# TensorE's turn re-ordered, and the routing counts moved to another PSUM bank

## The chip, the cores and the metric

The kernel runs on one core of a Trainium2 chip. The metric is the device time of one execution in microseconds (us), the median of three runs. The engines are named as the profile names them: PE (TensorE, matmuls), PEld (its weight loads), DVE (VectorE), ACT (ScalarE), POOL (GpSimd) and SP (the sync engine, which here issues DMAs).

## What is computed

The input holds 8 images of 16 x 16 tokens with 256 channels. Each image goes through a layer norm over channels, attention along rows and along columns (both of 16 tokens, the scores minus a squared distance) and an output projection, added to the image. Then 2048 tokens go through a mixture of 8 experts with one expert for each token: logits, argmax, a place in the expert's list of at most 256 tokens (the running count of earlier tokens that chose it), and an expert of 256 to 1024 to 256 with a ReLU, scaled by the gate and added.

```python
q, k, v = xn @ Wq.T + bq, xn @ Wk.T + bk, xn @ Wv.T + bv      # xn = layer norm of x
r = softmax(q.k along the row    - gw * dist) @ v
c = softmax(q.k along the column - gw * dist) @ v
x = x + (r + c) @ Wo.T + bo
t = layer norm of x; idx = argmax(t @ wg); mask = one_hot(idx)
loc = cumsum(mask, axis=0) - 1; mask = mask * (loc < C)       # C = 256
out = x + gate * (relu(t_e @ w1[e]) @ w2[e])                  # per expert e
```

## The kernel before

The program has three parts. A set-up (up to about 24 us) folds the weights. An attention part (about 24 to 76 us) takes the images one at a time, each as two tiles of 128 tokens. An expert part (from about 84 us) takes the experts one at a time. Products are made exact by splitting each operand into a high and a low part and running three passes (`three_passes`, lines 592 to 611), so each product needs a "high" copy from ACT and a "low" remainder from DVE.

Every engine has a queue written out by hand, in order, with semaphore waits between the engines. In the attention part one turn i (1 to 6) of the loop at L759 issues on PE:

- `transpose_x(i + 1)` (L622): the normalised image i+1 is transposed into `bank_xT`;
- `scores(i)`: needs the query of image i, high from ACT and low from DVE, and that DVE has read the previous scores;
- `transpose_prob(i - 1)` (L662): transposes the combined attention weights of image i-1 into `bank_pT`, after `weights_both(i - 1)` on DVE;
- `query(i + 1)`: needs the transposed image i+1, high from ACT, low from DVE (`x_low`);
- `counts(i - 2)` (L684 to L691): tiny matmuls that count earlier tokens by expert, into the tail of the bank `banks_v` half 0, after `choose(i - 2)` on DVE;
- `attention_out(i - 1, 0 and 1)` (L675): weights times values into `banks_o`;
- `values(i)`: values times output projection into `banks_v`, which needs ACT's copy of the values before and, as the counts lie in the same bank, that DVE has read the counts.

DVE's turn i (`turn`, L1235) is: `x_low(i + 1)` (L1118), `maxima(i)` for both tiles (L1170, L1173: masks the scores and takes their maxima), `place(i - 2)` (L1230 to L1233: reads the counts, gives `slot`), `first_norm(i + 4)` in turns 1 to 3 (L1105 to L1111: statistics of a later image), `weights_both(i)` (L1192 to L1196: reads the sums of ACT's exponentials, combines `e_col` and `e_row`), `query_low(i + 1)` (L1123), `residual(i - 1)` for both tiles (L1210: the new row of the output), and `choose(i - 1)` (L1218 to L1225: argmax of the logits, by way of `ranked` and `chosen`).

ACT's turn i (L977 to L987) is: `transposed_x(i + 1)`, `normalised_x(i + 2)`, `transposed_prob(i - 1)` (L916), `exponentials(i)` for both tiles (L929, L930), `query(i + 1)` (L910: the high part of the query), a piece of an expert's weights in some turns, `values(i)` (L936).

POOL's loop (L516) issues for image i: `pre_residual(i - 1)` (L466 to L470, four small operations), `x_and_bias(i)` (L476: image plus bias, which waits until `residual(i - 2)` has freed its buffer), in four turns a piece of `w1_low` (L492), `scatter_rows(i - 2)` (L483: two indirect DMAs that wait for `slot`), `sum_marks(i - 2)` (L502 to L505) and, while images are left, `first_rstd(i + 4)` (L428 to L431, which waits for `first_norm`). Ahead of the loop stand `x_and_bias(0)`, `pre_residual(0)`, `first_w1_low(2)`, `x_and_bias(1)`, `first_w1_low(3)` and `first_rstd(5)`; the first of these waits for `bias_rows` on DVE (L1164, L1165).

Of the kernel before, what the change touches and what calls it, by code (L numbers as in the profile page):

```python
# [39 lines left out]
E, F = 8, 1024  # L40
# [49 lines left out]
def wait(eng, sem, value):  # L90

    if isinstance(value, int) and value <= 0:
        return
    eng.wait_ge(sem, value)
# [18 lines left out]
def build(nc, x, Wq, bq, Wk, bk, Wv, bv, Wo, bo, sigma, wg, w1, w2, tables_in, eye, tokens, slots, out):  # L113
# [4 lines left out]
    with ctx:  # L118
# [93 lines left out]
        def halves(a):  # L212
            return a.rearrange("p (a b) -> p a b", a=2)
# [4 lines left out]
        ps_v, ps_o = two_banks("banks_v"), two_banks("banks_o")  # L218

        ps_count = halves(ps_v[:, 0, MW:MW + 2 * E])  # L220
        ps_x0 = [ps_q[:, 0, :], ps_s[:, 0, :]]
        ps_s_last = [ps_s[:, 0, :], ps_xT[:, 1, :]]
        ps_pT_last = [ps_pT, ps_q]
# [88 lines left out]

        def slot_of(i):
            return slot_last if i == B - 1 else slot[i % 2]


        def w1_high_count(e):
# [267 lines left out]
        def _(pe):  # L585
# [30 lines left out]
            def transpose_x(i):  # L616

                pe.wait_ge(xn_ready, i + 1)
                wait(pe, xT_ready, i)
                for t in range(2):  # L620
                    for c in range(DC):
                        step = nc.tensor.transpose(ps_xT[:, c, t * P:(t + 1) * P], xn[:, t, c * P:(c + 1) * P], ident)  # L622
                step.then_inc(xT_made, 1)
# [21 lines left out]
            def values(i, which=range(2)):  # L645

                j = i % 2
                wait(pe, v_ready, i)
                wait(pe, count_read, i - 1)
                for t in which:  # L650
                    step = three_passes(ps_v[:, t, 0:MW], [(xT_high[j][:, c, chunk[t]], xT_low[j][:, c, chunk[t]]) for c in range(DC)],
                                        [(m_high[:, c, :], m_low[:, c, :]) for c in range(DC)])
                    if t == 1 or i == B - 1:
                        step.then_inc(v_made, 1)

            def transpose_prob(i, which=range(2)):

                wait(pe, pT_ready, 2 * i)
                for t in which:
                    pe.wait_ge(u_ready, 2 * i + t + 1)  # L660
                    for c in range(2):
                        step = nc.tensor.transpose(pT_of(i, t)[:, c, t * P:(t + 1) * P], e_col[:, t, c * P:(c + 1) * P], ident)  # L662
                    step.then_inc(pT_made, 1)

            def attention_out(i, t, between=None):

                pe.wait_ge(pT_ready, 2 * i + (t + 1 if i == B - 1 else 2))
                pe.wait_ge(v_ready, i + 1 + (i == B - 1))
                wait(pe, x2_ready, 2 * (i - 1) + t + 1)
                if i == 0:  # L670
                    pe.wait_ge(b_ready, 1)
                for c in range(2):
                    if between and c:
                        between()
                    step = nc.tensor.matmul(ps_o[:, t, 0:VW], pT[:, c, t * P:(t + 1) * P], v_sb[i % 2][:, c, 0:VW], start=c == 0, stop=c == 1)  # L675
                step.then_inc(o_made, 1)

            def counts(i):

                pe.wait_ge(chosen_ready, i + 1)  # L680
                wait(pe, count_read, i)
                pe.wait_ge(v_ready, min(i + 2, B + 1))
                new, old = chosen_wide[i % 2], chosen_wide[1 - i % 2]
                nc.tensor.matmul(ps_count, ones[:, :], new[:, 0:2, :], start=True, stop=False)  # L684
                if i:
                    for t in range(2):
                        nc.tensor.matmul(ps_count, ones[:, :], old[:, 1 + t:2 + t, :].to_broadcast([P, 2, E]), start=False, stop=False)
                if i > 1:
                    pe.wait_ge(before_ready, i - 1)
                    nc.tensor.matmul(ps_count, ones[:, :], before[1 - i % 2][:, :].unsqueeze(1).to_broadcast([P, 2, E]), start=False, stop=False)  # L690
                nc.tensor.matmul(ps_count, upper, new[:, 1:3, :], start=False, stop=True).then_inc(count_made, 1)  # L691
# [16 lines left out]
            def fold_biases():  # L708

                pe.wait_ge(wide_ready, 1)  # L710
                for c in range(DC):
                    nc.tensor.matmul(ps_o[:, 1, 0:VW], bv_wide[:, c, :], woT[:, c, :], start=c == 0, stop=False)
                for c in range(DC):
                    step = nc.tensor.matmul(ps_ow, bo_wide[:, c, :], wgc[:, c, :], start=False, stop=c == DC - 1)
                step.then_inc(obias_made, 1)
# [40 lines left out]
            pe.wait_ge(m_ready, 1)  # L756
            values(0)
            fold_biases()
            for i in range(1, B - 1):  # L759
                transpose_x(i + 1)  # L760
                scores(i)
                transpose_prob(i - 1)
                query(i + 1)
                if i > 1:
                    counts(i - 2)
                attention_out(i - 1, 0)
                attention_out(i - 1, 1)
                values(i)


            transpose_prob(B - 2)
            scores(B - 1)
            counts(B - 3)
            attention_out(B - 2, 0)
# [100 lines left out]
        def _(act):  # L875
# [10 lines left out]
            def normalised_x(i):  # L886

                act.wait_ge(nmr_ready, x_group(i) + 1)
                wait(act, xT_made, i)
                for t in range(2):  # L890
                    r = 2 * i + t
                    step = nc.scalar.activation(xn[:, t, :], x_sb[:, r, :], ACT.Identity, scale=rstd[:, r:r + 1], bias=nmr[:, r:r + 1])
                step.then_inc(xn_ready, 1)
# [8 lines left out]
            def transposed_x(i):  # L902

                act.wait_ge(xT_made, i + 1)
                nc.scalar.activation(xT_high[i % 2][:, :, :], ps_xT, ACT.Copy).then_inc(xT_high_ready, 1)
# [27 lines left out]
            def values(i):  # L933
                act.wait_ge(v_made, i + 1)
                wait(act, pre_ready, i - 1)
                nc.scalar.activation(v_sb[i % 2][:, :, :], ps_v[:, :, 0:MW], ACT.Copy).then_inc(v_ready, 1)  # L936

            def second_w1_high(n):

                c, part = w1_piece(n)  # L940
                act.wait_ge(w1_in, 32)
                nc.scalar.activation(w1_high[1][:, c, part], w1_in_sb[:, c, part], ACT.Copy).then_inc(w1_high_ready, 1)
# [30 lines left out]
            normalised_x(2)  # L973
            query(1)
            values(0)
            for i in range(1, B - 1):
                transposed_x(i + 1)  # L977
                if i + 2 < B:
                    normalised_x(i + 2)
                transposed_prob(i - 1)  # L980
                exponentials(i)
                query(i + 1)
                if i + 1 in W1_TURNS:
                    second_w1_high(i + 1 - W1_TURNS[0])
                if i == B - 2:
                    split_w2(0, which=[0])
                values(i)  # L987


            def last_values(t):  # L990
# [98 lines left out]
        def _(dve):  # L1089
# [26 lines left out]
            def x_low(i):  # L1116
                dve.wait_ge(xT_high_ready, i + 1)
                low_part(xT_low[i % 2][:, :, :], ps_xT, xT_high[i % 2][:, :, :]).then_inc(xT_ready, 1)  # L1118
# [43 lines left out]
            def bias_rows():  # L1162
                dve.wait_ge(obias_made, 1)
                setup.mark(nc.vector.tensor_copy(ow[:, :], ps_ow))  # L1164
                nc.vector.tensor_tensor(obias[:, :], ps_obias, bo_sb[:, :], ALU.add).then_inc(b_ready, 1)  # L1165
# [61 lines left out]
            def place(i, target):  # L1227

                dve.wait_ge(count_made, i + 1)
                nc.vector.tensor_tensor(counted[:, :, :], ps_count, chosen[i % 2], ALU.mult).then_inc(count_read, 1)  # L1230
                dve.wait_ge(count_read, i + 1)
                route.done(nc.vector.tensor_reduce(loc[:, :], counted[:, :, :], axis=AX.X, op=ALU.add))
                return nc.vector.scalar_tensor_tensor(target[:, :], loc[:, :], float(E), rmax[:, :], ALU.mult, ALU.subtract)  # L1233

            def turn(i):  # L1235
                x_low(i + 1)
                maxima(i, 0)
                maxima(i, 1)
                if i > 1:
                    place(i - 2, slot_of(i - 2)).then_inc(slot_ready, 1)  # L1240
                if i < 4:
                    first_norm(i + 4)
                weights_both(i)
                query_low(i + 1)
                residual(i - 1, 0)
                residual(i - 1, 1)
                choose(i - 1)
# [9 lines left out]
            first_norm(4)  # L1257
            weights_both(0)
            query_low(1)
            bias_rows()  # L1260
            for i in range(1, B - 1):
                turn(i)
# [145 lines left out]
```

## Time and profile before

| what | us |
|---|---|
| median of 3 runs | 190.01 (190.01 to 190.08) |
| the profiled execution, its own time | 189.76 |
| its span, first to last instruction | 187.9 |
| PE busy | 175.9 (94%) |
| DVE busy | 147.6 (79%) |
| POOL busy | 119.6 (64%) |
| ACT busy | 112.8 (60%) |

The profiled execution lies 0.25 us under the median, and 1.86 us of it lie outside the span. In a timeline row the columns are: start (us from the span's start), length (us), engine, line, operation, output and inputs with their tile names, sizes, and the number of merged instructions; in square brackets the idle time before it and what ended it. The length of one row may reach a little into the next, since instructions overlap; the distance between starts is what a step takes of its engine's queue.

### The profile page before, as it was taken

The numbers are of one execution on the slowest core, as the hardware profiler recorded it, in microseconds if no ns is written. First come the engines' busy times: TensorE is split into PE (matmuls) and PEld (weight loads), VectorE is DVE, ScalarE is ACT, GpSimd is POOL, SyncE is SP. The second block draws the span as 40 slices with busy tenths as digits, with TensorE's granted clock in tenths as the row PEclk, the third lists the DMA queues.
The fourth block names the chain that finished last, engine by engine and source line by source line (L and its number), as shares of the span: only waits on it lengthen the run. The fifth ranks groups of instructions, "written<-read, shape, count | busy, mean of one in ns | idle before, by whom it ended". The sixth has DMA issues, their size and how long they took to land.

```text
span 187.9 us, 3937 instructions
## 1 busy us (share of the span) xinstructions
PE 175.9 (94%) x1370; PEld 168.8 (90%) x1370; DVE 147.6 (79%) x400; ACT 112.8 (60%) x273; POOL 119.6 (64%) x159
## 2 busy tenths in 40 slices
PE   7899999799999999989899899999999999999980
PEld 7788898699899999769899899999999999999970
DVE  1397979998987978755867889999699996997820
ACT  0647966578679488523659795791875926845000
POOL 4226778278877967828349688748468494369562
PEclk9999999999999999999999999999999999999996
DMA  5896997611312124769299629139184193601010
GB/s 169 244 368 226 301 258 205 234 61 58 112 36 85 58 86 124 244 179 304 53 330 356 236 79 390 36 127 345 62 284 162 63 348 145 205 22 45 5 68 30
DMA packets 23862, 31.67 MB, mean 169 GB/s; under 512 B 2729, under 2 KB 20650, under 8 KB 23841
## 3 DMA queue, kind: packets, MB, share of 16 engines
q1 hardware_dynamic: 20032, 26.01, 42.5%
q0 software_dynamic: 1616, 4.24, 6.4%
q10 hardware_dynamic: 2192, 1.16, 2.1%
q8 instruction: 11, 0.18, 0.4%
q14 instruction: 11, 0.08, 0.1%
HBM read 23.02 MB, written 8.55 MB: 168 GB/s over the span
## 4 chain that ended last, share of the span: by engine, by line
PE 65%; DVE 12%; DMA 10%; issue 5%; ACT 4%; SPq 2%; POOLq 1%; POOL 0%; DVEq 0%
PE banks_v L603 8%; PE banks_v L604 7%; PE banks_v L610 7%; DMA w_in_sb<-in_L_ffn_w 6%; PE banks_o L675 4%; PE bank_q L610 3%; PE bank_pT L610 3%; PE bank_pT L603 3%; PE bank_pT L604 3%; PE bank_s L610 3%; PE bank_s L603 3%; PE bank_s L604 3%; PE bank_q L603 3%; PE bank_q L604 3%; DMA slots<-row,slot 2%
## 5 line engine op out<-in xcount | busy, mean ns | idle before, releaser
L950 ACT ACTIVATE w_high<-w_in_sb 128x1024 fp32r<-128x1024 f32 x22 | 22.9, 1057 | 4.2 <-DMA w_in_sb<-in_L_ffn_w 4.0
L560 POOL DMA_INDIRECT out<-y,goal x16 | 16.7, 1041 | 11.6 <-issue 5.8
L483 POOL DMA_INDIRECT slots<-row,slot x14 | 14.3, 1023 | 14.7 <-DVE slot L1233 8.8
L542 POOL TENSOR_TENSOR w_low<-vx,w_high 128x1024 fp32r<-128x1024 f32 x8 | 20.1, 2532 | 5.2 <-ACT w_high L950 5.2
L542 POOL TENSOR_TENSOR w_low<-w_in_sb,w_high 128x1024 fp32r<-128x1024 f32 x7 | 16.7, 2409 | 9.7 <-ACT w_high L950 9.6
L1322 DVE TENSOR_TENSOR w_low<-w_in_sb,w_high 128x1024 fp32r<-128x1024 f32 x12 | 15.8, 1317 | 5.1 <-ACT w_high L950 4.7
L603 PE MATMUL banks_v<-w_high,h_high 128*128 128x256 f32 x64 | 16.3, 291 | 0.5 <-issue 0.5
L675 PE MATMUL banks_o<-vx,pT 128*128 128x266 f32 x64 | 16.4, 397 | 0.3 <-issue 0.3
L1048 ACT ACTIVATE h_high<-bank_xT 128x512 fp32r<-128x512 f32 x8 | 4.8, 594 | 18.6 <-PE bank_xT L610 18.6
L604 PE MATMUL banks_v<-w_high,h_low 128*128 128x256 f32 x64 | 15.8, 283 | 0.0
L603 PE MATMUL bank_pT<-w_high,h_high 128*128 128x256 f32 x56 | 14.0, 287 | 0.0
L604 PE MATMUL bank_pT<-w_high,h_low 128*128 128x256 f32 x56 | 13.7, 283 | 0.0
L675 PEld LDWEIGHTS banks_o<-vx,pT 128*128 128x128 f32 x64 | 11.4, 189 | 2.1 <-issue 0.5
L603 PEld LDWEIGHTS banks_v<-w_high,h_high 128*128 128x128 f32 x64 | 12.2, 191 | 0.9 <-POOL w_low L542 0.7
L1337 DVE TENSOR_TENSOR gate_g<-ginv,rstd_g 128x2 f32<-128x2 f32 x8 | 12.5, 1567 | 0.3
L1339 DVE CAST goal<-sl 128x2 int32<-128x2 f32 x8 | 12.2, 1522 | 0.3
L604 PEld LDWEIGHTS banks_v<-w_high,h_low 128*128 128x128 f32 x64 | 12.3, 192 | 0.0
L476 POOL TENSOR_TENSOR vx<-sl,obias 128x512 f32<-128x512 f32 x8 | 10.3, 1288 | 1.7 <-DVE obias L1165 1.3
L1105 DVE BATCH_NORM_STATS2 stats<-sl 128x6 f32<-128x256 f32 x16 | 6.0, 416 | 6.2 <-DMA sl<-in_x 6.1
L604 PEld LDWEIGHTS bank_pT<-w_high,h_low 128*128 128x128 f32 x56 | 10.8, 192 | 0.0
L603 PEld LDWEIGHTS bank_pT<-w_high,h_high 128*128 128x128 f32 x56 | 10.7, 192 | 0.0
L603 PE MATMUL banks_v<-m_high,xT_high 128*128 128x274 f32 x32 | 10.3, 339 | 0.3 <-DVE m_low L1114 0.3
(239 smaller groups left out, 658.1 us busy)
## 6 DMA issues: line engine op xcount, KB each, us to landing
w_in_sb<-in_L_ffn_w SPq DMA_DIRECT2D x12, 1024.0 KB, 6.6
vx<-in_L_ffn_w SPq DMA_DIRECT2D x4, 1024.0 KB
sl<-slots SPq DMA_DIRECT2D x9, 266.0 KB, 4.2
slots<-empty SPq DMA_DIRECT2D x8, 266.0 KB, 4.1
sl<-in_x SPq DMA_DIRECT2D x8, 256.0 KB, 8.9
out<-row SPq DMA_DIRECT2D x7, 256.0 KB
table_in<-in_tables ACTq DMA_DIRECT2D x1, 292.0 KB, 8.3
w_in_sb<-in_L_conv_Wq ACTq DMA_DIRECT2D x1, 256.0 KB, 4.0
```

The source lines that it names most:

```text
L476: nc.gpsimd.tensor_tensor(xb[i % 2][:, :, 0:D], x_sb[:, tiles(i), :], obias[:, None, :].to_broadcast([P, 2, D]), ALU.add).then_inc(xb_read ...
L483: nc.gpsimd.indirect_dma_start(slot_rows, bass.IndirectOffsetOnAxis(ap=slot_of(i)[:, t:t + 1].bitcast(u32), axis=0), row_of(i)[:, t, :], N ...
L542: step = nc.gpsimd.tensor_tensor(w2_low[e % 2][:, half, :], w2_raw[e % 2][:, half, :], w2_high[e % 2][:, half, :].bitcast(f32), ALU.subtract)
L560: nc.gpsimd.indirect_dma_start(out_rows, bass.IndirectOffsetOnAxis(ap=goal[j][:, c:c + 1].bitcast(u32), axis=0), y[j][:, c, :], None, boun ...
L603: nc.tensor.matmul(out_ap, a_h, b_h, start=c == 0, stop=False)
L604: nc.tensor.matmul(out_ap, *second, start=False, stop=False)
L610: step = nc.tensor.matmul(out_ap, *third, start=False, stop=c == n - 1)
L675: step = nc.tensor.matmul(ps_o[:, t, 0:VW], pT[:, c, t * P:(t + 1) * P], v_sb[i % 2][:, c, 0:VW], start=c == 0, stop=c == 1)
L950: nc.scalar.activation(high[e % 2][:, half, :], raw[:, half, :], ACT.Copy).then_inc(ready, 1)
L1322: step = nc.vector.tensor_tensor(w1_low[e % 2][:, c, :], w1_in_sb[:, c, :], w1_high[e % 2][:, c, :].bitcast(f32), ALU.subtract)
L1337: gate.done(nc.vector.tensor_tensor(gate_g[:, tiles(e)], ginv[:, tiles(e)], rstd_g[:, tiles(e)], ALU.mult))
L1339: nc.vector.tensor_copy(goal[j][:, :], sl[:, tiles(e), COL_TOK]).then_inc(goal_ready, 1)
```

## The change

On PE the turn becomes: scores(i), query(i+1), counts(i-2), values(i), transposes of x(i+2), attention_out(i-1), transposes of the weights of image i. The transposes of a later image thus come a whole turn sooner than they are used, and the weights of image i are transposed at the end of its own turn and not in the middle of the next. The counts of images 0 to 4 go to the tail of `banks_o` half 1, so `values` no longer waits for DVE's reading of the counts, and the second `attention_out` does instead. ACT and DVE are re-ordered with it: ACT takes `transposed_x(i + 2)` after the query and `normalised_x(i + 3)` last; DVE takes `query_low(i + 1)` ahead of `weights_both(i)`, both ahead of `first_norm(i + 4)`, and then `x_low(i + 2)`; `x_low(2)` moves ahead of the loop and ahead of `bias_rows`.

```diff
+        ps_count_turn = halves(ps_o[:, 1, VW:VW + 2 * E])
...
+        def count_of(i):
+            return ps_count if i >= B - 3 else ps_count_turn
@@ values
                 wait(pe, v_ready, i)
-                wait(pe, count_read, i - 1)
+                if i == B - 1:
+                    pe.wait_ge(count_read, i - 1)
@@ attention_out
                 wait(pe, x2_ready, 2 * (i - 1) + t + 1)
+                if t == 1 and i < B - 2:
+                    wait(pe, count_read, i)
@@ counts
                 wait(pe, count_read, i)
-                pe.wait_ge(v_ready, min(i + 2, B + 1))
+                if i >= B - 3:
+                    pe.wait_ge(v_ready, min(i + 2, B + 1))
+                ps_count = count_of(i)
@@ the queue of PE
             fold_biases()
+            transpose_x(2)
             for i in range(1, B - 1):
-                transpose_x(i + 1)
                 scores(i)
-                transpose_prob(i - 1)
+                if i == 1:
+                    transpose_prob(0)
                 query(i + 1)
                 if i > 1:
                     counts(i - 2)
+                values(i)
+                if i + 2 < B:
+                    transpose_x(i + 2)
                 attention_out(i - 1, 0)
                 attention_out(i - 1, 1)
-                values(i)
-
-
-            transpose_prob(B - 2)
+                transpose_prob(i)
@@ the queue of ACT
             values(0)
+            transposed_x(2)
+            normalised_x(3)
             for i in range(1, B - 1):
-                transposed_x(i + 1)
-                if i + 2 < B:
-                    normalised_x(i + 2)
                 transposed_prob(i - 1)
                 exponentials(i)
                 query(i + 1)
                 if i + 1 in W1_TURNS:
                     second_w1_high(i + 1 - W1_TURNS[0])
+                if i + 2 < B:
+                    transposed_x(i + 2)
                 if i == B - 2:
                     split_w2(0, which=[0])
                 values(i)
+                if i + 3 < B:
+                    normalised_x(i + 3)
@@ the queue of DVE
             def turn(i):
-                x_low(i + 1)
                 maxima(i, 0)
                 maxima(i, 1)
                 if i > 1:
                     place(i - 2, slot_of(i - 2)).then_inc(slot_ready, 1)
+                query_low(i + 1)
+                weights_both(i)
                 if i < 4:
                     first_norm(i + 4)
-                weights_both(i)
-                query_low(i + 1)
+                if i + 2 < B:
+                    x_low(i + 2)
                 residual(i - 1, 0)
                 residual(i - 1, 1)
                 choose(i - 1)
...
             query_low(1)
+            x_low(2)
             bias_rows()
```

`place` reads `count_of(i)` where it read `ps_count`.

## Rows read from the trace of the kernel before

**Rows 1.** Busy time by stretch: us, then PE, PEld, DVE, ACT, POOL; clock, DMA

```profile
23.92:69.84 45.92, 44.29 (x335) 41.73 (x335) 40.30 (x162) 32.84 (x92) 34.25 (x63) 1.00 0.38 117
62.55:69.84 7.29, 7.29 (x59) 6.96 (x58) 5.86 (x26) 5.13 (x14) 5.68 (x11) 1.00 0.22 79
```

**Rows 2.** Timeline of PE, first matmul of each step of turn 6

```profile
62.90 0.36 PE L603 MATMUL bank_s<-xT_high,qT_high 128*128 128x256 f32 x1
...
64.42 0.60 PE L662 MATMUL bank_pT<-ident,e_col 128*128 128x128 f32 x4
64.78 0.36 PE L603 MATMUL bank_q<-xT_high,a_high 128*128 128x256 f32 x1
...
66.42 2.04 PE L675 MATMUL banks_o<-vx,pT 128*128 128x266 f32 x8
68.10 0.48 PE L603 MATMUL banks_v<-m_high,xT_high 128*128 128x274 f32 x1
```

**Rows 3.** Timeline of DVE, steps of turn 2 from its maxima on

```profile
35.40 0.41 DVE L1170 CUSTOM_DVE_ANT_0 s_col<-bank_s,mask_col 128x256 f32<-128x256 f32 x1
...
37.32 0.74 DVE L1105 BATCH_NORM_STATS2 stats<-sl 128x6 f32<-128x256 f32 x2
...
38.55 0.17 DVE L1192 RECIPROCAL einv<-esum 128x4 f32<-128x4 f32 x1
...
39.48 0.87 DVE L1123 SCALAR_TENSOR_TENSOR qT_low<-bank_q,qbias,qT_high 128x256 fp32r<-128x256 f32 x2
40.27 0.89 DVE L1210 SCALAR_TENSOR_TENSOR row<-banks_o,einv,vx 128x266 f32<-128x266 f32 x2
...
41.40 0.36 DVE L1220 SCALAR_TENSOR_TENSOR ranked<-row,lmax,table_in 128x8 f32<-128x8 f32 x2
...
42.09 0.68 DVE L1114 TENSOR_TENSOR xT_low<-bank_xT,xT_high 128x512 fp32r<-128x512 f32 x1
```

**Rows 4.** Timeline of ACT, first exponential and query of turn 2

```profile
36.13 0.51 ACT L929 ACTIVATE e_col<-s_col,ntop 128x256 f32<-128x256 f32 x1 [1.63 <-DVE ntop L1173]
...
37.90 0.81 ACT L910 ACTIVATE qT_high<-bank_q,qbias 128x256 fp32r<-128x256 f32 x2
```

**Rows 5.** Timeline of all engines, POOL beside DVE's choice at the end of turn 1

```profile
33.03 1.28 POOL L476 TENSOR_TENSOR vx<-sl,obias 128x512 f32<-128x512 f32 x1 [0.40 <-DVE row L1210]
...
33.12 1.34 DVE L1220 SCALAR_TENSOR_TENSOR ranked<-row,lmax,table_in 128x8 f32<-128x8 f32 x2
...
34.80 0.68 DVE L1114 TENSOR_TENSOR xT_low<-bank_xT,xT_high 128x512 fp32r<-128x512 f32 x1
```

**Rows 6.** Timeline of POOL, steps of turns 1, 2 and 4

```profile
27.83 1.26 POOL L476 TENSOR_TENSOR vx<-sl,obias 128x512 f32<-128x512 f32 x1
29.06 1.27 POOL L447 TENSOR_TENSOR w_low<-w_in_sb,w_high 128x512 fp32r<-128x512 f32 x1
...
40.96 0.73 POOL L428 TENSOR_TENSOR rstd<-var_eps,minus_half 128x2 f32<-128x2 f32 x1
...
42.07 0.22 POOL L466 TENSOR_TENSOR vx<-vx,std 128x16 f32<-128x16 f32 x1
...
54.07 1.05 POOL L483 DMA_INDIRECT slots<-row,slot  x1 [0.89 <-DVE slot L1233]
...
56.87 0.22 POOL L466 TENSOR_TENSOR vx<-vx,std 128x16 f32<-128x16 f32 x1
...
57.49 1.30 POOL L476 TENSOR_TENSOR vx<-sl,obias 128x512 f32<-128x512 f32 x1
```

**Rows 7.** Timeline of DVE, ahead of turn 1 and image 7's first maxima

```profile
24.19 0.41 DVE L1165 TENSOR_TENSOR obias<-banks_o,bo_sb 128x256 f32<-128x256 f32 x1
25.23 0.69 DVE L1114 TENSOR_TENSOR xT_low<-bank_xT,xT_high 128x512 fp32r<-128x512 f32 x1 [0.62 <-ACT xT_high L905]
...
71.35 0.42 DVE L1170 CUSTOM_DVE_ANT_0 s_col<-bank_s,mask_col 128x256 f32<-128x256 f32 x1 [0.18 <-PE bank_s L610]
```

**Rows 8.** Chain of waits behind the attention part: start, us, what

```profile
75.03 4.53 DMA slots<-row,slot
```

More of the change, by code:

```diff
@@ L1229, in place @@
                 dve.wait_ge(count_made, i + 1)
-                nc.vector.tensor_tensor(counted[:, :, :], ps_count, chosen[i % 2], ALU.mult).then_inc(count_read, 1)
+                nc.vector.tensor_tensor(counted[:, :, :], count_of(i), chosen[i % 2], ALU.mult).then_inc(count_read, 1)
                 dve.wait_ge(count_read, i + 1)
```

## The prediction

> **What bounds the kernel now.** I read the busy time by stretch first, then the timelines of PE, DVE, ACT and POOL over the attention part, then the chain of waits behind it. From 23.92 to 69.84 us PE is busy 44.29 of 45.92 us, at a granted clock of 1.00 (the 2.4 GHz level), and in turn 6 for all its 7.29 us [rows 1]. So PE bounds these six turns, and 45.92 - 44.29 = 1.63 us is all that any order of its work can win there. The steps of turn 6, from start to start: scores 1.52, transposes of the weights 0.36, query with counts 1.64, output 1.68, values up to 69.84 1.74, transposes of x 62.55 to 62.90 0.35; sum 7.29 [rows 1, 2].
>
> DVE is busy 40.30 of the 45.92 us [rows 1], which looks like room. The reader is to see in the DVE timeline that its queue is also a ring: maxima of image i, which ACT's exponentials wait for, then steps that wait for ACT, then the maxima of the next image, in one order [rows 3, 4]. The length of that ring, waits included, decides whether PE stays the bound. Behind the attention part the last scatter's DMA and the experts' work follow one after another [rows 8], so what the attention part gains or loses reaches the end nearly whole; I take it as whole.
>
> **The change part by part.**
>
> *PE.* No matmul is added or removed: the work of a turn stays 7.29 us. At best the 1.63 us go.
>
> *DVE's ring.* Durations from turn 2, start to start [rows 3]: weights 0.93 (38.55 to 39.48), query_low 0.79 (39.48 to 40.27), both residuals and the choice 1.82 (40.27 to 42.09), first_norm 1.23 (37.32 to 38.55); x_low 0.60 (34.80 to the maxima at 35.40) [rows 3, 5]. ACT's first exponential starts 0.73 after the maxima (36.13 - 35.40), the four exponentials take 1.77 (36.13 to 37.90) and the query 0.81 [rows 3, 4]. So the exponentials are done 2.50 after the maxima and the query 3.31 after them.
>
> Before, DVE spent this wait on place and first_norm, took the weights at 38.55, 3.15 after the maxima, and the query was ready when DVE came to query_low. In the new order query_low stands first. It needs ACT's query, so DVE can't go on before 3.31, and place is all that it has until then; first_norm, which filled the gap, now stands behind. Counted from the maxima: query_low to 4.10, weights to 5.03, first_norm to 6.26, x_low to 6.86, residuals and choice to **8.68** in turns 1 to 3. Turns 4 and 5 have no first_norm: **7.45**. Turn 6 has no x_low either: **6.85**. All but the last are longer than PE's 7.29. PE doesn't hold the ring up: the transposes of the weights can start at 5.03, then 0.36, then the first half of the next scores (0.76): 6.15 after the maxima, before DVE comes back to them. So DVE becomes the bound and PE waits for it, at the counts (for the choice) and at the transposes of the weights.
>
> *The start.* x_low(2) still starts at 25.23, but ahead of bias_rows: 25.23 + 0.60 + some 0.42 for the pair (its longer one is 0.41) = 26.25 for the first maxima [rows 3, 5, 7]. Without any collision image 7's maxima, at 71.35 before [rows 7], would come at 26.25 + 3 x 8.68 + 2 x 7.45 + 6.85 = 74.04, so +2.7 us.
>
> *Collisions with POOL.* In turn 1 of before, POOL's x_and_bias starts at 33.03, as soon as the residual frees its buffer, DVE's `ranked` starts at 33.12, and the pair that takes 0.36 elsewhere takes 1.34: it ends with POOL's operation (33.03 + 1.28 = 34.31), and the next step starts 0.49 after that, at 34.80 [rows 3, 5]. In later turns of before POOL was late: in turn 2 it reached pre_residual at 42.07, when the choice was over (42.09) [rows 3, 6]. Now DVE's turn is longer and POOL is early. In turns 4 and 5 place ends by 2.0 after the maxima (first_norm follows it at 37.32 - 35.40 = 1.92 [rows 3]); scatter starts some 0.87 later (0.89 idle in its row), 2.80 from scatter to pre_residual and 0.62 to x_and_bias [rows 6] make 6.3, and the residual's end, 0.09 ahead of `ranked` at 5.63 + 1.13 = 6.76, is later (1.13 is 41.40 - 40.27 [rows 3]): POOL waits ready and starts at 6.67, ends at 7.95, the turn ends 0.49 later, 8.44 and not 7.45. In turns 2 and 3 POOL first waits for first_norm (6.26, some 0.17 to be seen), then 1.11 for first_rstd (40.96 to 42.07) and 0.62: 8.16, when one `ranked` has run (7.99) and the second or `chosen` is next. It ends at 9.44; with the rest of the choice, some 0.4, 9.85. In turn 6 POOL is ready at 6.3, `ranked` due at 6.16: again in the midst of the choice, 6.3 + 1.28 + 0.35 = 7.9.
>
> The Trainium skill (SBUF — State Buffer, "Who interferes with whom") says that a DVE instruction with two inputs in SBUF contends with a GpSimd instruction that reads SBUF, and that the one issued first holds the pair while the other blocks whole. The trace agrees for `ranked` (1.34 against 0.36). By that rule an operation of DVE that is issued first would go free in the ties of turns 2, 3 and 6, but `chosen`, also from SBUF, would then be caught; either way the turn ends with POOL's operation.
>
> *Turn 1.* The weights there start at 26.25 + 4.10 = 30.35. bias_rows comes 1.72 later than before (24.19 to 25.91), POOL with it, so x_and_bias(1) runs from 29.55 to 30.78 and first_w1_low(3) from 30.78 to 32.05 [rows 6, 7]. No row of before shows `e_col` beside a POOL operation. Its cost lies between nothing and waiting for both, 1.3 us (32.05 + 0.53 for its two instructions = 32.58 in place of 31.28). I take 1.3, since the nearest row is `ranked`, the same kind of operation with both inputs in SBUF [rows 5]. Then first_norm to 33.81, x_low to 34.41; POOL 33.98, 35.09, x_and_bias 35.71 to 36.99, again in the choice: the turn ends at 37.4, 11.15 long.
>
> *Edits at nothing.* The second output matmul's new wait for the counts: place is done by 2.0, the output's second half comes behind counts (at the turn's start), values, transposes and a first half, 0.1 + 1.74 + 0.35 + 0.84 = 3.0; without that cover it costs at most 0.5 per turn, with the transposes of the weights queued behind it. `values` without its wait: nothing, that wait isn't seen to end late before. The transposes of x and ACT's two steps for them: used a turn later. No DMA is moved in a queue; SP's place_row and the second w1 load start some 1.7 later behind bias_rows and first_w1_low(3) and are used many us after.
>
> **The sum.** 26.25 + 11.15 + 2 x 9.85 + 2 x 8.44 + 7.9 = 81.9 for image 7's maxima, against 71.35: **+10.5**. The profiled execution would take 189.76 + 10.5 = 200.3; it lies 0.25 under the median, so **200.5** by the median.
>
> **The rivals.**
> *The ring without most collisions.* If POOL and DVE miss each other, +2.7: 192.7. With the two of turn 1 alone (1.3 + 1.2) it is 195.2; with half of them about 196.5. For it: the ties of turns 2, 3 and 6 hang on 0.2 us, and one row carries the price. Against: whatever starts first, POOL's start is released by the residual that the choice follows.
> *Faster: PE stays the bound.* If ACT's query came early enough that DVE's turn stayed under 7.29 (it decides at query_low: 1.4 us earlier in turns 1 to 3, 0.2 in 4 and 5), the new order would remove PE's waits: 190.01 - 1.63 = 188.4. For it: DVE is busy only 40.30 of 45.92 us. Against: the wait for ACT can't be filled in a queue kept in order.
> *No change*: slack at the end, where the scatter's DMA of 4.53 follows [rows 8], swallows it; nothing in the chain offers that much: 190.0.
> *Slower still.* PE would be busy 7.29 of about 9.85; if the granted clock fell to the 1.2 GHz level, its turn would be 14.6 and the time over 220. Against: the granted clock is 1.00 in both stretches, and the gaps would be near 1.2 us each [rows 1].
>
> **How the numbers follow.** Forecast (198.5 to 202.5) 0.56; ring with few or some collisions (192.6 to 198.5) 0.29; PE the bound, 188.4, 0.08; no change 0.03; over 202.5 0.04. The range 192.6 to 202.5 takes the first two, 0.85. Faster by over 0.2% 0.08, within 0.2% (about what a measurement of this kernel tells from no change) 0.03, slower 0.89.
>
> **What would show it.** Right: in the DVE timeline a wait of over 1 us for ACT's query after place in each turn; PE idle before counts and before the transposes of the weights, released by DVE; turns of 8.4 to 10 us between maxima; `ranked` or `chosen` of some 1.3 us beside x_and_bias; image 7's maxima near 82. Wrong: PE busy throughout and turns of 7.3 (the ring isn't the bound), or turns of 8.7 and 7.5 with `ranked` at 0.36 (no collisions).

## The result

The changed kernel takes 202.94 us (median of 4 runs, 202.60 to 203.39) against 190.05 us for the kernel before (four runs; 190.01 by the first three alone): a ratio of 1.0689 with a 95% interval of [1.0653, 1.0724], 12.9 us slower. The forecast was 200.5 us with a range up to 202.5; the direction and the mechanism hold, the size was 2.4 us too small. The profiled execution took 203.22 us with a span of 201.4, 13.5 more than the 187.9 of before.

The page's busy times of the changed kernel: PE does the same 1370 matmuls, and its share fell from 94 to 88%.

```profile
PE 177.4 (88%) x1370; PEld 168.3 (84%) x1370; DVE 152.2 (76%) x400; ACT 112.5 (56%) x273; POOL 120.5 (60%) x159
```

Busy time by stretch in the changed kernel, first over the attention part from the transposes of x(2) to image 7's maxima, then turn by turn, from one image's maxima on DVE to the next (columns as in rows 1):

```profile
24.69:86.31 61.62, 46.87 (x349) 42.10 (x348) 48.11 (x168) 34.57 (x95) 37.53 (x70) 1.00 0.31 94
```

```profile
26.86:37.78 10.92, 8.79 (x66) 7.99 (x64) 8.44 (x30) 5.76 (x16) 8.54 (x16) 1.00 0.78 226
37.78:48.41 10.63, 7.48 (x54) 6.69 (x54) 8.62 (x33) 5.65 (x16) 6.42 (x12) 1.00 0.18 62
48.41:59.03 10.62, 7.54 (x56) 6.75 (x56) 8.60 (x33) 5.65 (x16) 6.67 (x14) 1.00 0.15 52
59.03:68.69 9.66, 7.56 (x57) 6.77 (x57) 7.71 (x27) 5.65 (x16) 5.74 (x11) 1.00 0.16 56
68.69:78.34 9.65, 7.57 (x57) 6.78 (x57) 7.70 (x26) 4.70 (x14) 5.70 (x10) 1.00 0.16 56
78.34:86.31 7.97, 5.76 (x41) 4.96 (x41) 6.02 (x26) 5.59 (x14) 4.45 (x9) 1.00 0.18 61
```

The kernel before does the same stretch, up to image 7's maxima at 71.35 [rows 7], with 348 matmuls and 45.80 us of busy PE. So PE's work is within 1.1 us of what it was, and now it stands beside 15 us of waiting; the granted clock stays at 1.00 (the 2.4 GHz level) with PE busy 70 to 80% of a turn. Who waited for whom in this part (us in total, times, longest):

```profile
DVE qT_low L1138 <- ACT qT_high L922: 10.6, 6, 2.2
PE banks_o L693 <- DVE chosen L1240: 8.6, 5, 2.3
PE bank_pT L667 <- DVE e_col L1211: 5.3, 6, 1.3
```

DVE waits for ACT's query in each of six turns, 1.8 us a time, and PE waits for DVE at the two places that the prediction named, the counts (the row of `banks_o`, where the counts now lie) and the transposes of the weights (`bank_pT`). The timeline of DVE in turn 4 answers to [rows 3]:

```profile
59.03 0.41 DVE L1185 CUSTOM_DVE_ANT_0 s_col<-bank_s,mask_col 128x256 f32<-128x256 f32 x1
...
60.54 0.16 DVE L1248 SCALAR_TENSOR_TENSOR slot<-loc,rmax 128x2 int32<-128x2 f32 x1
62.37 0.88 DVE L1138 SCALAR_TENSOR_TENSOR qT_low<-bank_q,qbias,qT_high 128x256 fp32r<-128x256 f32 x2 [1.67 <-ACT qT_high L922]
63.17 0.17 DVE L1207 RECIPROCAL einv<-esum 128x4 f32<-128x4 f32 x1
...
64.09 0.69 DVE L1129 TENSOR_TENSOR xT_low<-bank_xT,xT_high 128x512 fp32r<-128x512 f32 x1
64.69 0.89 DVE L1225 SCALAR_TENSOR_TENSOR row<-banks_o,einv,vx 128x266 f32<-128x266 f32 x2
...
65.83 2.46 DVE L1235 SCALAR_TENSOR_TENSOR ranked<-row,lmax,table_in 128x8 f32<-128x8 f32 x2
...
68.69 0.42 DVE L1185 CUSTOM_DVE_ANT_0 s_col<-bank_s,mask_col 128x256 f32<-128x256 f32 x1
```

query_low starts 3.34 after the maxima (3.31 forecast), the weights 4.14 (4.10), x_low 5.06 (5.03), the residual 5.66 (5.63). Up to here the ring is as reckoned. Then the two `ranked` take 2.46 us in place of 0.36, where 1.34 was forecast. POOL in the same stretch shows why:

```profile
65.73 1.31 POOL L480 TENSOR_TENSOR vx<-sl,obias 128x512 f32<-128x512 f32 x1 [0.59 <-DVE row L1225]
66.98 1.28 POOL L496 TENSOR_TENSOR w_low<-w_in_sb,w_high 128x512 fp32r<-128x512 f32 x1
```

Two operations stand in a row, x_and_bias and the piece of `w1_low` behind it. The first `ranked` is held to the end of the first, the second to the end of the second (65.83 + 2.46 = 68.29; 66.98 + 1.28 = 68.26). In turn 2 the first `ranked` goes ahead of POOL, the second is held by x_and_bias, and `chosen` by `w1_low`; first DVE, then POOL:

```profile
45.80 1.46 DVE L1235 SCALAR_TENSOR_TENSOR ranked<-row,lmax,table_in 128x8 f32<-128x8 f32 x2
47.29 0.17 DVE L1237 TENSOR_REDUCE rmax<-ranked 128x2 f32<-128x16 f32 x1
47.50 0.99 DVE L1240 TENSOR_TENSOR chosen<-table_in,rmax 128x16 bf16<-128x16 bf16 x1
```

```profile
45.97 1.27 POOL L480 TENSOR_TENSOR vx<-sl,obias 128x512 f32<-128x512 f32 x1
47.19 1.27 POOL L496 TENSOR_TENSOR w_low<-w_in_sb,w_high 128x512 fp32r<-128x512 f32 x1
```

`rmax` between them, with a single input, takes its 0.17 us beside POOL's second operation and is not held.

### The profile page after: what moved, and what is told of

Its sections match the earlier page's. It is cut to its first block, busy times and chain, and to the rows that moved or that the text cites. A ratio compares the mean times of both kernels' runs of the same rounds, so it can differ in the third digit from the quotient of the medians.

```text
span 201.4 us, 3936 instructions
## 1 busy us (share of the span) xinstructions
PE 177.4 (88%) x1370; PEld 168.3 (84%) x1370; DVE 152.2 (76%) x400; ACT 112.5 (56%) x273; POOL 120.5 (60%) x159
## 3 DMA queue, kind: packets, MB, share of 16 engines
q10 hardware_dynamic: 2192, 1.16, 2.0%
## 4 chain that ended last, share of the span: by engine, by line
PE 52%; DVE 22%; ACT 11%; DMA 6%; issue 4%; SPq 2%; POOLq 1%; DVEq 0%; ACTq 0%
PE banks_v L607 6%; PE banks_v L608 6%; DMA w_in_sb<-in_L_ffn_w 6%; PE banks_v L614 6%; DVE ranked L1235 5%; ACT e_col L941 4%; PE bank_pT L614 3%; PE bank_pT L607 3%; PE bank_pT L608 3%; DVE qT_low L1138 3%; DVE row L1225 2%; ACT e_row L942 2%; ACT qT_high L922 2%; PE banks_o L682 2%; DVE e_col L1211 2%
## 5 line engine op out<-in xcount | busy, mean ns | idle before, releaser
L941 ACT ACTIVATE e_col<-s_col,ntop 128x256 f32<-128x256 f32 x16 | 8.1, 503 | 24.0 <-DVE ntop L1188 23.9
L1138 DVE SCALAR_TENSOR_TENSOR qT_low<-bank_q,qbias,qT_high 128x256 fp32r<-128x256 f32 x16 | 7.0, 478 | 10.6 <-ACT qT_high L922 10.6
L432 POOL TENSOR_TENSOR rstd<-var_eps,minus_half 128x2 f32<-128x2 f32 x8 | 5.7, 707 | 11.3 <-DVE var_eps L1126 11.3
L1235 DVE SCALAR_TENSOR_TENSOR ranked<-row,lmax,table_in 128x8 f32<-128x8 f32 x14 | 11.0, 827 | 0.2
```

Source lines behind the costliest of these rows:

```text
L941: nc.scalar.activation(e_col[:, t, :], s_col[:, t, :], ACT.Exp, bias=ntop[:, t, 0:1], scale=-1.0, accum_out=esum[j][:, t:t + 1])
L1138: step = nc.vector.scalar_tensor_tensor(qT_low[:, d, :], ps_q[:, d, :], qbias[:, d:d + 1], qT_high[:, d, :].bitcast(f32), ALU.add, ALU.sub ...
L1235: route.mark(nc.vector.scalar_tensor_tensor(ranked[:, t, :], logits[:, t, :], lmax[:, t:t + 1], rank[:, t, :], ALU.is_equal, ALU.mult))
```

## The experiments

The theory: DVE's ring is the bound, made long by `query_low` ahead of the weights and by `first_norm` out of the gap, and each turn's end is held by POOL. The rivals: PE's new order or the counts' new bank costs; the collisions are everything; they are nothing. Times are medians, ratios stand against the kernel before on the same chip. A turn's length runs from the first maxima on DVE to the next image's, in the profiled execution. The bare ring is the ring as reckoned without collisions.

### The middle of DVE's turn undone

```diff
-                query_low(i + 1)
-                weights_both(i)
                 if i < 4:
                     first_norm(i + 4)
+                weights_both(i)
+                query_low(i + 1)
                 if i + 2 < B:
                     x_low(i + 2)
```

> The kernel after, with only the middle of DVE's turn as before: first_norm, weights, query_low, and x_low of the later image behind them; PE's and ACT's new queues and the counts' new bank stay. Theory (DVE's ring, made long by query_low ahead of weights and first_norm, is the bound): from the maxima, weights at 2.54 or, with first_norm, about 3.0, query_low done by 4.3 to 4.7, choice by 6.7 to 7.1, under PE's 7.29; PE is the bound again, the six turns take about 7.3 each, 188 to 191 us. Rival 1 (PE's new order or the counts in the other bank is what costs): still 198 us or more. Rival 2 (collisions with POOL alone make the loss): they come with POOL being early, which this edit changes little, so 196 or more, with turns of over 8.5.

Measured: 191.32 us, 1.0058 [1.0027, 1.0089]. Of the 12.9 us all but 1.3 are gone with PE's and ACT's new queues and the counts' new bank still in place, so neither of those is what costs. It is a little over the expected range. Turns 2 to 6 take 7.04, 7.85, 6.85, 6.86 and 6.27, but turn 1 takes 10.65. There first_norm's last two steps and `ratio` are held by three POOL operations in a row (29.27 to 33.01), which start behind bias_rows; DVE in turn 1:

```profile
29.37 1.21 DVE L1125 TENSOR_SCALAR minus_mean<-mean_var 128x2 f32<-128x2 f32 x1
30.50 1.31 DVE L1126 TENSOR_SCALAR var_eps<-mean_var 128x2 f32<-128x2 f32 x1
...
31.92 1.10 DVE L1208 TENSOR_TENSOR ratio<-esum,einv 128x2 f32<-128x2 f32 x1
```

`minus_mean` and `var_eps` read one tensor each, so it is not only operations with two inputs in SBUF that are held. In turn 2 of the changed kernel they take 0.17 and 0.16 us.

### DVE's new order alone, in the kernel before

```diff
-                if i < 4:
-                    first_norm(i + 4)
-                weights_both(i)
                 query_low(i + 1)
+                weights_both(i)
+                if i < 4:
+                    first_norm(i + 4)
                 residual(i - 1, 0)
```

> The kernel before, with one edit on DVE: query_low ahead of weights, both ahead of first_norm; the queues of PE, ACT and POOL and the counts' bank as before. Theory (the ring): 8.7 us and 7.5 us a turn without collisions, about 10.6 and 9.7 with them; 196 to 203 us, most of the loss without any change to PE. Rival 1 (PE's new order or the counts' bank costs): 190 to 191 us.

Measured: 198.72 us, 1.0424 [1.0326, 1.0522]. About two thirds of the loss (8.7 of 12.9 us by the medians, 0.62 of it by the ratios) come with no change to PE, ACT, POOL or the bank. Turns 1 to 3 take 8.87, 8.78 and 8.76, the bare ring of 8.68; turns 4 and 5 take 9.42 and 9.80, with the choice held again (`ranked` takes 2.58 us in turn 5). The wait for the query, in turn 4:

```profile
56.20 0.88 DVE L1123 SCALAR_TENSOR_TENSOR qT_low<-bank_q,qbias,qT_high 128x256 fp32r<-128x256 f32 x2 [1.27 <-ACT qT_high L910]
```

### POOL's second operation taken away

```diff
-                step = nc.gpsimd.tensor_tensor(w1_low[1][:, c, part], w1_in_sb[:, c, part], w1_high[1][:, c, part].bitcast(f32), ALU.subtract)
+                few = slice(part.start, part.start + 8)
+                step = nc.gpsimd.tensor_tensor(w1_low[1][:, c, few], w1_in_sb[:, c, few], w1_high[1][:, c, few].bitcast(f32), ALU.subtract)
```

The rest of `w1_low[1]` is set to zero by POOL at the program's start.

> The kernel after, with POOL's four pieces of the second expert's weight remainder cut to 8 columns each (the rest of that remainder is left out and stays zero). Theory: in turns 2 to 5 the choice on DVE is caught by two POOL operations in a row, x_and_bias and this one; without the second, turns 2 and 3 go from 10.6 to about 9.85 and turns 4 and 5 from 9.66 to about 8.45: 4.0 us less, 198.5 to 199.5. Rival (the second piece hides behind the first): under 1 us less, 202 or more.

Measured: 199.43 us, 1.0514 [1.0440, 1.0589], 3.5 us under the changed kernel. Turns 2 to 5 take 9.92, 9.87, 8.59 and 8.59: the 9.85 and 8.44 of the prediction, to 0.15. In turn 4 `ranked` is held once:

```profile
64.12 1.38 DVE L1239 SCALAR_TENSOR_TENSOR ranked<-row,lmax,table_in 128x8 f32<-128x8 f32 x2
```

So the second catch is what the prediction's turns 2 to 5 lacked, but for 0.4 us in the four together.

### Both of POOL's operations taken away

```diff
-                nc.gpsimd.tensor_tensor(xb[i % 2][:, :, 0:D], x_sb[:, tiles(i), :],
-                                        obias[:, None, :].to_broadcast([P, 2, D]), ALU.add).then_inc(xb_ready, 1)
+                nc.gpsimd.tensor_tensor(xb[i % 2][:, :, 0:8], x_sb[:, tiles(i), 0:8],
+                                        obias[:, None, 0:8].to_broadcast([P, 2, 8]), ALU.add).then_inc(xb_ready, 1)
```

This stands on top of the edit before it; the rest of `xb` starts at zero, so most of the image is left out of the sum that the residual adds.

> The kernel after, with the same pieces cut and POOL's sum of image and bias cut to 8 columns for every image (the rest of that sum is left out). Theory: the ring alone is left, 8.7 us in turns 1 to 3 (turn 1 may keep up to 1 us of a collision with the first expert's pieces), 7.45 in turns 4 and 5, 6.85 in turn 6: image 7's maxima about 12 us sooner than in the kernel after, 190.5 to 194. Rival 1 (collisions are everything and the ring is no bound): 188 to 189, turns of 7.3. Rival 2 (collisions cost little, the ring is longer than reckoned): 198 or more.

Measured: 192.35 us, 1.0127 [1.0065, 1.0189]. The turns are 8.85, 8.83, 8.84, 7.57, 7.57 and 6.98, the ring of 8.68, 7.45 and 6.85 to 0.17. In turn 4 POOL's small operation starts as before the choice, and `ranked` has its 0.36:

```profile
59.36 0.22 POOL L484 TENSOR_TENSOR vx<-sl,obias 128x16 f32<-128x16 f32 x1 [0.59 <-DVE row L1230]
59.45 0.36 DVE L1240 SCALAR_TENSOR_TENSOR ranked<-row,lmax,table_in 128x8 f32<-128x8 f32 x2
```

By these two kernels the ring without POOL's work loses 2.35 us, the first operation 7.1 more and the second 3.5 more, together 12.9. (The split is not a strict one: the kernel before has collisions of its own in turn 1.)

### first_norm alone back in the gap

```diff
+                if i < 4:
+                    first_norm(i + 4)
                 query_low(i + 1)
                 weights_both(i)
-                if i < 4:
-                    first_norm(i + 4)
```

> The kernel after, with first_norm alone moved back into the gap that DVE has behind place; query_low stays ahead of weights. Theory (ring and collisions): the ring of turns 2 and 3 becomes that of turns 4 and 5 (first_norm's 1.23 us lie beside the wait for ACT's query), so these two turns go from 10.6 to about 9.65, and turn 1 stays near 10.6, as first_norm's last two steps then stand beside POOL's first pieces; turns 4 to 6 unchanged: 200.3 to 201.5 us. Rival (the two operations that stand in the wrong order are what costs, first_norm's place is nothing): 202.5 or more.

Measured: 198.68 us, 1.0466 [1.0424, 1.0508]: more of a gain than expected (200.3 to 201.5). The turns are 9.87, 9.47, 8.42, 9.64, 9.66 and 7.97. The rival falls, but the size was wrong too: turn 3 was to be 9.65. POOL's x_and_bias came later there than the two `ranked`, so only `chosen` was held, once (1.02 us), and `w1_low` ran beside the maxima, which weren't held. Turn 1 gained 1.05 where I had expected some 0.3.

### The weights alone ahead of the query again

```diff
-                query_low(i + 1)
                 weights_both(i)
+                query_low(i + 1)
                 if i < 4:
                     first_norm(i + 4)
```

> The kernel after, with weights ahead of query_low again; first_norm stays behind both. Theory: weights no longer wait for the query (2.54 in place of 4.10 after the maxima), query_low ends at 4.3 in place of the weights' 5.03, so each of six turns gets 0.77 us shorter; the collisions at the choice stay: turns 2 and 3 about 9.85, 4 and 5 about 8.9, turn 6 about 7.3; 197.5 to 199.5 us. Rival (only first_norm's place counts, the swap costs nothing): 202.5 or more.

Measured: 200.41 us, 1.0551 [1.0509, 1.0593]. Turns 2 to 6 are 9.91, 9.93, 8.93, 8.93 and 7.14, each 0.7 to 0.8 shorter than in the changed kernel, as expected. Turn 1 is 0.56 longer, 11.48: the weights now come beside two of POOL's first pieces, and `e_col` is held for 2.61 us. That is why the time lies over the expected range.

### The counts' bank alone, in the kernel before

```diff
-                wait(pe, count_read, i - 1)
+                if i == B - 1:
+                    pe.wait_ge(count_read, i - 1)
...
+                if t == 1 and i < B - 2:
+                    wait(pe, count_read, i)
...
+                ps_count = count_of(i)
```

> The kernel before, with the counts of images 0 to 4 in the other bank alone: values no longer wait for the reading of the counts, the second output matmul does; all orders as before. Theory: neither wait ends last, 190.0 us within 0.3%. In this order the output follows the counts at once, and the second half comes some 0.9 us behind them, while place ends some 0.6 us after the counts: up to 0.3 us a turn if that is tighter than reckoned, 191.5 at most. Rival (the bank is what costs): 195 or more.

Measured: 190.31 us, 1.0015 [0.9990, 1.0041]. The bank is worth nothing either way: each turn is within 0.04 us of the kernel before.

### x_low ahead of the choice, in the kernel before

```diff
-                x_low(i + 1)
+                if i not in (2, 4):
+                    x_low(i + 1)
                 maxima(i, 0)
...
                 residual(i - 1, 1)
+                if i in (1, 3):
+                    x_low(i + 2)
                 choose(i - 1)
```

> The kernel before, with x_low of images 3 and 5 ahead of the choice on DVE and not behind it; nothing else. In the kernel before PE waits 1.63 us in all, for these two. Theory: both waits go, the counts wait instead for a choice that ends 0.6 us later, about 0.5 us in turn 2: 188.6 to 189.4 us. Rival (DVE's turn is the bound there as well, the wait only moves to the counts): 189.8 to 190.3.

Measured: 188.41 us, 0.9923 [0.9894, 0.9951]: faster than the kernel before, and 0.2 us under the expected range. The rival falls. PE's waits for x_low shrink from 1.6 us to 0.3, and the attention part is PE's own work; busy time from the transposes of x(2) to image 7's maxima:

```profile
24.20:69.96 45.76, 45.46 (x348) 43.16 (x348) 41.36 (x167) 34.24 (x95) 35.41 (x68) 1.00 0.40 123
```

### PE's new order with DVE's old one, bias_rows first

The first experiment's kernel, with one more edit:

```diff
-            x_low(2)
             bias_rows()
+            x_low(2)
```

> The first experiment's kernel (the middle of DVE's turn as before, PE's and ACT's new queues kept), with bias_rows ahead of x_low(2) on DVE, as in the kernel before. That experiment still lost in turn 1 alone: 10.65 us, with minus_mean, var_eps, ratio and ranked each held for some 1.2 us by POOL, whose first pieces start with bias_rows. Theory: POOL starts 0.7 us or more earlier, ratio goes free, turn 1 falls to 9.2 to 9.6 as in the kernel before, PE waits some 0.6 us for the first counts in place of 2.0 in all: 188.8 to 190.0 us. Rival (PE's new order itself costs about 1 us, the collisions of turn 1 hide behind it): 190.8 to 191.6.

Measured: 188.64 us, 0.9940 [0.9909, 0.9971]. This is 0.2 us under the expected range. Turn 1 falls from 10.65 to 9.02, though not as expected: `ratio` is still held (1.04 us), and it is `var_eps` that goes free (0.15). PE is busy 45.46 of 46.15 us:

```profile
23.90:70.05 46.15, 45.46 (x350) 42.64 (x349) 43.26 (x168) 33.96 (x95) 35.24 (x65) 1.00 0.40 119
```

So PE's new order costs nothing in itself. With the middle of DVE's turn and bias_rows as they were, and x_low still ahead of the choice, it is a little faster than the kernel before. Beside it on the same chip ran the kernel of the last section again:

> The kernel before with x_low of images 3 and 5 ahead of the choice, again, on the chip of this call, beside the other: a comparison of the two orders of PE at their best. Theory: PE waits under 0.5 us in it, so the two differ by no more than the waits left: 188.2 to 189.4 us. Rival (its gain was that of one chip): 189.7 to 190.3.

Measured: 188.77 us, 0.9934 [0.9905, 0.9964]. The two can't be told apart: once PE's waits are gone, either order of PE's work gives the same time.

## Why the prediction was too small

Term by term, in us, the profiled executions:

| term | forecast | measured |
|---|---|---|
| first maxima of turn 1 | 26.25 | 26.86 |
| turn 1 | 11.15 | 10.92 |
| turns 2 and 3, each | 9.85 | 10.63, 10.62 |
| turns 4 and 5, each | 8.44 | 9.66, 9.65 |
| turn 6 | 7.9 | 7.97 |
| maxima of image 7 | 81.9 | 86.31 |
| from there to the end of the span | 116.55 | 115.1 |

*Right: PE's work is unchanged and DVE's ring is the bound.* The bare ring was forecast as 8.68, 7.45 and 6.85 and measured as 8.8, 7.57 and 6.98 with POOL's work taken away. The undone middle of DVE's turn brings the time back, and the same edit in the kernel before takes it away.

*Right: the collision of turn 1.* The weights' `e_col` take 1.59 us and not 0.61, so 0.98 us more where 1.3 was forecast, beside POOL's `first_w1_low(3)`, which runs from 31.40 to 32.67 (DVE, then POOL):

```profile
31.50 1.59 DVE L1211 SCALAR_TENSOR_TENSOR e_col<-e_row,ratio,e_col 128x128 f32<-128x128 f32 x2
```

```profile
31.40 1.27 POOL L451 TENSOR_TENSOR w_low<-w_in_sb,w_high 128x512 fp32r<-128x512 f32 x1
```

So `e_col` is held as `ranked` is, which no row of before showed. The Trainium skill's rule of two inputs in SBUF (SBUF — State Buffer, "Who interferes with whom") agrees with this row. In the ties of turns 2 and 3 it came out as that page of the Trainium skill says too: the first `ranked`, 0.17 us ahead of POOL, ran, and the second was held. One row further down does not fit it.

*Wrong: "the turn ends with POOL's operation".* The step that failed is the price of the collision at the choice in turns 2 to 5. The sum held one POOL operation against each choice. In those four turns POOL has a piece of `w1_low` right behind x_and_bias, and the choice has three operations with both inputs in SBUF, two `ranked` and `chosen`. Each of the two POOL operations catches one of them: `ranked` and `chosen` in turns 2 and 3, both `ranked` in turns 4 and 5 (2.46 us, where 1.34 was forecast). Turns 2 and 3 came out 0.78 and 0.77 longer than forecast, 4 and 5 1.22 and 1.21, 4.0 us in all, and with `w1_low` cut to 8 columns they are within 0.15 of the forecast. The rows could have shown it: `w1_low` stands in POOL's loop in just these turns, and two POOL operations with no gap between them are in [rows 6].

*Wrong, the other way: "I take it as whole".* From image 7's maxima to the end 1.46 us came back. Some 0.63 lie ahead of the experts. Before, the scatter's DMA and the load behind it [rows 8] ended last, 11.34 us after those maxima (82.69); now the load is there after 8.53 us (94.84), and PE's own work and image 7's `place` on DVE end last. The chain of before, behind the line in [rows 8]:

```profile
79.63 3.03 DMA sl<-slots
82.69 0.52 ACT xs L1003
```

Another 0.69 lie in the first expert; first matmul of its hidden layer and of its output, changed kernel:

```profile
99.08 0.36 PE L607 MATMUL bank_xT<-xg_high,w_high 128*128 128x256 f32 x1 [0.34 <-ACT xg_high L1034]
...
105.14 0.28 PE L607 MATMUL banks_v<-w_high,h_high 128*128 128x256 f32 x1
```

and the output's first matmul in the kernel before, where the hidden layer starts at 84.75:

```profile
91.50 0.36 PE L603 MATMUL banks_v<-w_high,h_high 128*128 128x256 f32 x1 [0.53 <-issue]
```

The wait of 0.53 is gone. The trace of before shows what ended it. The output's first matmul waits, among others, for a piece of the second layer's weight remainder on DVE; that piece ran beside POOL's own piece of it (DVE, then POOL):

```profile
87.93 3.47 DVE L1295 TENSOR_TENSOR w_low<-w_in_sb,w_high 128x512 fp32r<-128x512 f32 x1
```

```profile
88.42 2.42 POOL L542 TENSOR_TENSOR w_low<-w_in_sb,w_high 128x1024 fp32r<-128x1024 f32 x1
```

The same operation on the piece before takes 0.69 us at 82.42, with no POOL operation beside it. Here it ends at 91.40, 0.56 behind POOL's end, and the matmul starts 0.10 later. In the changed kernel it ends at 103.59, 0.56 behind POOL again, but PE comes for it only at 105.14. In the seven kernels in which PE finds this piece unfinished it idles 0.50 to 0.53 us there, in the other five not at all. So this wait, too, was a collision, and the changed kernel hides it. In the row of before DVE starts 0.49 us ahead of POOL and is held all the same, which the Trainium skill's rule that the one issued first runs (same section) does not give. An indirect DMA of POOL's (87.43, 0.98 us) was still running at that start; whether it matters, no run separates. The remaining 0.3 us I can't place.

*The start.* The first maxima of turn 1 are 0.61 late, but image 0's, which the change doesn't reach, are 0.63 late already (18.70 against 18.07), so this is the set-up's own spread and not the change (over all the kernels run, image 0's first maxima lie between 17.87 and 19.03). It is in the 13.5 us between the two profiled spans: 0.61 + 3.82 (the six turns together) - 1.46 = 2.97 over the forecast's 10.53. The turns alone were forecast 3.82 us too short. That the total missed by less, 2.97 in the spans and 2.4 by the medians, is luck: the end gave back more than the start took, and the prediction foresaw neither.

*The rivals.* The ring alone was priced at 192.7, and the kernel with both of POOL's operations cut takes 192.35. Faster with PE as the bound was right about the size: 188.4 was forecast for a kernel without PE's waits, and two kernels with under 0.7 us of them took 188.41 to 188.77. The condition named for it, a turn of DVE that `query_low` does not hold up, is the edit that gets there from the changed kernel, together with bias_rows. The time lies over 202.5 because of the second catch and not because of the clock, which stayed at 1.00 in all six turns.

## What to carry to other kernels

Before an in-order queue is re-ordered, write down its ring: the steps from one wait to the same wait of the next turn, with every wait for another engine in it. An engine that is busy 78% of the time (DVE here, 48.11 of 61.62 us) can be the bound, and an operation that fills a wait is worth up to its whole length there (first_norm, 1.23 us long, made turn 2 1.16 us shorter when it went back into the gap). Count the collisions between DVE and POOL by pairs: of small operations with both inputs in SBUF that follow one another, each POOL operation in an unbroken row can hold one more, and a POOL operation that is released by a DVE step starts just when the steps behind it come.

## What the runs showed of the hardware

A DVE operation of 0.2 us with both inputs in SBUF that meets POOL's 1.27 us is held to POOL's end (`chosen`, 0.99 us in place of 0.17), and two in a row were held by two, 2.46 us in place of 0.36. Held, too, were `minus_mean` and `var_eps`, with one input (1.21 and 1.31). Not held were `rmax`, with one input (0.17), and maxima, with one input in PSUM (0.41 us, in the kernel with first_norm in the gap). When POOL's operation was 16 columns wide in place of 512, the same start beside `ranked` cost nothing (0.36). The granted clock stayed at 1.00 through six turns in which PE was busy 70 to 80% and waited up to 2.3 us at a time.
